# Statistics of x1 in the scan of a Mamba layer: VectorE's bn_stats per row chunk against two accumulating passes on ScalarE

## What is computed

```python
x = x + _L0_conv_ref(_gn(x), ...)     # Mamba: in_proj, conv, selective scan, gate, out_proj
x = x + _L1_conv_ref(_gn(x), m)       # memory of 1024 rows: assign, segment sums, soft read-out

def _gn(v, G=32, eps=1e-5):
    g = v.reshape(B_, G, C_ // G, H_, W_)
    m = jnp.mean(g, axis=(2, 3, 4), keepdims=True)
    s = jnp.var(g, axis=(2, 3, 4), keepdims=True)
    return ((g - m) / jnp.sqrt(s + eps)).reshape(v.shape)
...
def step(h, inp):                     # the selective scan, d = 1024 channels, 16 states
    u_t, d_t, b_t, c_t = inp
    dA = jnp.exp(d_t[..., None] * A)
    dBu = (d_t * u_t)[..., None] * b_t[:, None, :]
    h = dA * h + dBu
    y = jnp.einsum('bdn,bn->bd', h, c_t)
```

## Time and profile before

| | |
|---|---|
| median of 3 runs | 4616.05 us (4615.56 to 4617.21) |
| the profiled execution | 4618.12 us, its span 4616.3 us |
| `scan`: first scan to last gate | 952.64 to 3487.01 us of the span |
| granted clock of TensorE | 0.99 over the span |
| statistics in `scan` (L887) | 64 instructions, 667 ns median |

### The profile page before, as it was taken

The page is one execution under the profiler, slowest core; times in us unless marked ns, Lnnn a source line. Parts: engine busy times, 40 slices in busy tenths (PEclk is TensorE's granted clock), DMA queues, the critical chain, the costliest instruction groups (busy, mean ns, idle before and its releaser), DMA issues. The chain is left out here.

```text
span 4616.3 us, 110600 instructions
## 1 busy us (share of the span) xinstructions
PE 4401.1 (95%) x47036; PEld 2940.8 (64%) x47036; DVE 3880.4 (84%) x4033; ACT 2863.4 (62%) x6005; POOL 2932.5 (64%) x1321
## 2 busy tenths in 40 slices
PE   5999999968999999999999999999997999999999
PEld 4777777745555555555555555555554778777887
DVE  5877677689999999999999999999995777777332
ACT  2666676667777777777777777777763444443111
POOL 1223333269999999999999999999993222222000
PEclk9999999989999999999999999999998999999999
DMA  3555455442233323333332333233321212212543
GB/s 149 207 204 190 165 188 197 170 149 88 84 102 100 100 84 94 100 93 94 102 101 80 96 103 101 83 101 98 97 76 64 83 56 82 83 55 119 199 184 146
DMA packets 195258, 538.60 MB, mean 117 GB/s; under 512 B 15600, under 2 KB 15616, under 8 KB 185680
## 3 DMA queue, kind: packets, MB, share of 16 engines
q1 hardware_dynamic: 189888, 482.41, 31.6%
q0 software_dynamic: 4880, 49.12, 2.7%
HBM read 329.09 MB, written 202.38 MB: 115 GB/s over the span
## 5 line engine op out<-in xcount | busy, mean ns | idle before, releaser
L996 POOL TENSOR_TENSOR sc_hc<-sc_hc,sc_c_rep 128x1024 f32<-128x1024 f32 x1024 | 2390.3, 2383 | 127.0 <-ACT sc_state L1009 102.3
L1191 DVE TENSOR_TENSOR_SCAN sc_hc<-l_m,sc_state,sc_ring 128x512 f32<-128x512 f32 x2048 | 2419.0, 1254 | 11.5 <-PE sc_ring L1118 5.8
L1041 ACT ACTIVATE l_m<-l1s_v,l_neg_a 128x512 f32<-128x512 f32 x2048 | 1351.5, 707 | 6.9 <-DMA l1s_v<-spill 6.8
L1118 PEld LDWEIGHTS sc_ring<-sc_diag,l1s_iota 64*64 64x64 f32 x32768 | 898.5, 133 | 458.4 <-issue 453.2
L1118 PE MATMUL sc_ring<-sc_diag,l1s_iota 64*64 64x128 f32 x32768 | 1042.8, 274 | 45.1 <-DVE sc_hc L1191 41.1
L1128 PE MATMUL sc_y_ps<-sc_hc,sc_fold 128*64 128x512 f32 x4096 | 936.1, 599 | 0.9 <-POOL sc_hc L996 0.9
L1009 ACT ACTIVATE sc_state<-sc_hc 128x2 f32<-128x2 f32 x1024 | 207.1, 202 | 626.0 <-DVE sc_hc L1191 625.8
L1128 PEld LDWEIGHTS sc_y_ps<-sc_hc,sc_fold 128*64 128x64 f32 x4096 | 271.5, 136 | 484.9 <-issue 461.9
L1460 POOL TENSOR_TENSOR l_count<-l_count,as_oh 128x1024 f32<-128x1024 f32 x64 | 184.0, 2875 | 523.4 <-DVE as_oh L1656 523.4
L879 PE MATMUL sc_o_ps<-l_et,l_sums 128*128 128x512 f32 x960 | 464.0, 606 | 4.4 <-ACT sc_b_col L1019 4.4
L70 PE MATMUL fr_mm<-fr_xn_hi,l0f_w_in_hi 128*128 128x512 f32 x1024 | 407.9, 398 | 15.3 <-DVE fr_xn_lo L676 8.6
(11 more groups left out here) (185 smaller groups left out, 5731.1 us busy)
## 6 DMA issues: line engine op xcount, KB each, us to landing
sc_duz<-spill SPq DMA_DIRECT2D x128, 768.0 KB, 6.1
l1s_v<-spill SPq DMA_DIRECT2D x256, 256.0 KB, 4.0
spill<-fr_z SPq DMA_DIRECT2D x64, 512.0 KB, 3.5
spill<-fr_u SPq DMA_DIRECT2D x32, 1024.0 KB, 5.9
spill<-fr_delta SPq DMA_DIRECT2D x32, 1024.0 KB, 5.2
spill<-fr_du SPq DMA_DIRECT2D x32, 1024.0 KB, 6.3
sc_c_rep<-bc SPq DMA_DIRECT2D x128, 256.0 KB, 4.4
soft<-l_et SPq DMA_DIRECT2D x16, 2048.0 KB, 6.2
```

What stands on the lines that cost most here:

```text
L996: nc.gpsimd.tensor_tensor(hc[:, p], hc[:, p], c_rep[:, 2 * q:2 * q + 2, :], ALU.mult).then_inc(s_hp, 1)
L1041: nc.scalar.activation(da[:, p % 4, r, :], delta[:, i % 2, p % 2, :], ACT.Exp, scale=keep.neg_a[:, c:c + 1]).then_inc(s_da, 1)
L1118: done = nc.tensor.matmul(to[:, :, k::4], dut[rows, i % 2, k, HALF * h:HALF * h + HALF], diag[rows, u, 4 * q + c:4 * q + 4:2, k, :], start ...
L1191: nc.vector.tensor_tensor_scan(hc[:, p, r, :], da[:, p % 4, r, :], ring[:, SLOT[at], r::2], state[:, i, 2 * p + r:2 * p + r + 1], ALU.mult ...
```

## The change

In the blocks of `scan` VectorE takes no statistics any more. ScalarE takes them in two steps at the same places of the loops (odd blocks, same tiles m): after the decays of p = 2 the sum over the tile's 512 tokens by an Identity pass with the accumulator (`chunk_mean`), followed by two copies of one column (the mean, and the shift for the next step), and after the decays of p = 5 the sum of squares about that mean by a Square pass with the accumulator (`chunk_variance`), which also raises `s_res`. Both passes write their unused full output to `o_sb`. The five last statistics stay on VectorE, each a `bn_stats` followed by a `bn_aggr` of its own. `keep.mv` holds a mean and a variance for every chunk, and `group_params` puts the second norm's from these by twelve small VectorE instructions that add halves, in place of the eight `bn_aggr`. The first group norm is unchanged.

```diff
-        def statistics(dve, b, j, m):
-            g = b * NJ + j
-            dve.wait_ge(s_sum, KC * g + m + 1)
-            nc.vector.bn_stats(keep.stats[:, b * KC + m, j, :], x_res[:, m % 2, :]).then_inc(s_res, 1)
+        def chunk_mean(act, b, j, m):
+            n = KC * (b * NJ + j) + m
+            act.wait_ge(s_sum, n + 1)
+            nc.scalar.activation(o_sb[:, m % 2, :], x_res[:, m % 2, :], ACT.Identity, accum_out=total[:, 0:1]).then_inc(s_total, 1)
+            act.wait_ge(s_total, n + 1)
+            nc.scalar.activation(keep.mv[:, b * KC + m, j, 0:1], total[:, 0:1], ACT.Copy, scale=1.0 / T).then_inc(s_mean, 1)
+            nc.scalar.activation(total[:, 1:2], total[:, 0:1], ACT.Copy, scale=-ROOT / T).then_inc(s_mean, 1)
+
+        def chunk_variance(act, b, j, m):
+            n = KC * (b * NJ + j) + m
+            act.wait_ge(s_mean, 2 * n + 2)
+            nc.scalar.activation(o_sb[:, m % 2, :], x_res[:, m % 2, :], ACT.Square, bias=total[:, 1:2], scale=ROOT,
+                                 accum_out=keep.mv[:, b * KC + m, j, 1:2]).then_inc(s_res, 1)
+
+        def last_statistics(dve, b, j, m):
+            n = KC * (b * NJ + j) + m
+            dve.wait_ge(s_sum, n + 1)
+            nc.vector.bn_stats(keep.stats[:, m, j, :], x_res[:, m % 2, :]).then_inc(s_taken, 1)
+            dve.wait_ge(s_taken, n - KC * (NG - 1) + 2)
+            nc.vector.bn_aggr(keep.mv[:, b * KC + m, j, :], keep.stats[:, m, j, :]).then_inc(s_res, 1)
...
                             decays(g, i, p)
+                            for at, part in ((2, chunk_mean), (5, chunk_variance)):
+                                if p == at and i in (3, 5, 7) and past:
+                                    part(act, *past[0], i // 2 - 1)
+                                if p == at and i == 1 and len(past) > 1:
+                                    part(act, *past[1], KC - 1)
...
                             recur(g, i, p, 1)
-                            if p == 3 and i in (3, 5, 7) and past:
-                                statistics(dve, *past[0], i // 2 - 1)
-                            if p == 3 and i == 1 and len(past) > 1:
-                                statistics(dve, *past[1], KC - 1)
...
+                def add_halves(t, count, before):
+                    while count > 1:
+                        count //= 2
+                        dve.wait_ge(halved, before)
+                        nc.vector.tensor_tensor(t[:, :, 0:count], t[:, :, 0:count], t[:, :, count:2 * count], ALU.add).then_inc(halved, 1)
+                        before += 1
+                    dve.wait_ge(halved, before)
+
+                nc.vector.tensor_copy(part[:], of_chunks).then_inc(halved, 1)
+                add_halves(part, NJ, 1)
+                nc.vector.scalar_tensor_tensor(away[:], of_chunks[:, :, :, 0], float(NJ), part[:, :, 0:1, 0].broadcast_to([P, n, NJ]),
+                                               ALU.mult, ALU.subtract).then_inc(halved, 1)
+                dve.wait_ge(halved, 5)
+                nc.vector.tensor_tensor(away[:], away[:], away[:], ALU.mult).then_inc(halved, 1)
+                add_halves(away, NJ, 6)
+                nc.vector.scalar_tensor_tensor(mv[:, :, 1], away[:, :, 0], 1.0 / NJ ** 2, part[:, :, 0, 1], ALU.mult,
+                                               ALU.add).then_inc(halved, 1)
```

More of the change, by code:

```diff
@@ L72, in split_matmul, with group_params @@
     return nc.tensor.matmul(out, lhs[0], rhs[1], start=False, stop=stop)
-def group_params(nc, tag, keep, stats, scale, shift, early=()):
+def group_params(nc, tag, keep, stats, scale, shift, early=(), of_chunks=None):
     n = stats.shape[1]
@@ L88, in group_params @@
         step = w.sem("step")
+        halved = w.sem("halved")
+        part = w.sb("part", [P, n, NJ, 2])
+        away = w.sb("away", [P, n, NJ])
         mean_ps = w.sem("mean_ps")
@@ L100, in _ @@
         def _(dve):
-            for i in range(n):
-                nc.vector.bn_aggr(mv[:, i, :], stats[:, i, :, :]).then_inc(step, 1)
-            dve.wait_ge(step, n)
+            if of_chunks is None:
+                for i in range(n):
+                    nc.vector.bn_aggr(mv[:, i, :], stats[:, i, :, :]).then_inc(step, 1)
+                dve.wait_ge(step, n)
+            else:
+                def add_halves(t, count, before):
[14 more added lines that the diff above has]
+                                               ALU.add).then_inc(halved, 1)
+                dve.wait_ge(halved, 10)
+                nc.vector.tensor_scalar(mv[:, :, 1], mv[:, :, 1], 1.0 / NJ, None, ALU.mult).then_inc(step, n - 1)
+                nc.vector.tensor_scalar(mv[:, :, 0], part[:, :, 0, 0], 1.0 / NJ, None, ALU.mult).then_inc(step, 1)
+                dve.wait_ge(step, n)
             nc.vector.tensor_copy(mean[:], mv[:, :, 0]).then_inc(step, 1)
@@ L797, in scan @@
     DIAGS = (1, 1, 1, 2, 2, 1, 1, 0)
+    ROOT = T ** -0.5
     with ExitStack() as ctx:
@@ L808, in scan @@
         o_ps = w.ps("o_ps", [P, T])
+        total = keep.total
         s_w = w.sem("w_out_loaded")
@@ L835, in scan @@
         s_res = w.sem("x1_done")
+        s_total = w.sem("x1_totalled")
+        s_mean = w.sem("x1_mean_done")
+        s_taken = w.sem("last_x1_taken")
         st_x1 = [w.sem(f"x1_stored{i}") for i in range(2)]
@@ L1322, in low @@
                                             ALU.subtract).then_inc(s_lo, 1)
-                statistics(dve, NB - 1, NJ - 2, KC - 1)
+                last_statistics(dve, NB - 1, NJ - 2, KC - 1)
                 dve.wait_ge(s_root, 1)
@@ L1332, in _ @@
                 for m in range(3):
-                    statistics(dve, NB - 1, NJ - 1, m)
+                    last_statistics(dve, NB - 1, NJ - 1, m)
                 for n in range(4):
                     low(n)
-                statistics(dve, NB - 1, NJ - 1, 3)
+                last_statistics(dve, NB - 1, NJ - 1, 3)
                 for n in range(4, 8):
@@ L1855, in program @@
         keep.stats = w.sb("stats", [P, NB * KC, NJ, 6])
+        keep.mv = w.sb("mv", [P, NB * KC, NJ, 2])
+        keep.total = w.sb("total", [P, 2])
         keep.scale = w.sb("scale", [P, NB * KC])
@@ L1895, in program @@
                     scan(nc, keep, d)
-                    group_params(nc, "g2", keep, keep.stats[:], keep.scale[:], keep.shift[:])
+                    group_params(nc, "g2", keep, keep.stats[:], keep.scale[:], keep.shift[:], of_chunks=keep.mv[:])
                     assign(nc, keep, d)
```

## The result

The changed kernel takes 4583.58 us (median of 4 executions, 4578.80 to 4587.27), the kernel before 4616.63 us beside it (4 executions, 4615.56 to 4617.39). The ratio is 0.9928, 95% interval 0.9916 to 0.994: 33 us or 0.72% faster. The profiled execution is the slowest of the four, 4587.27 us, with a span of 4585.5 us. Two executions further down, 6811 us in experiment 7 (the profiled one, mean granted clock 0.61) and 6181 us in experiment 9 (0.68), are in no median and no comparison.

The account below looks back on a forecast made before the run. VectorE was taken to set the pace of `scan`. −34.5 + 0.25 + 0.6 = −33.65 us against the profiled 4618.12 us gave 4584.5, and with the median 2.07 us lower 4582.4 us; range 4579 to 4603 us.

Parts of the forecast that it names:

- VectorE sets the pace, 59 × 0.585 us: In `scan`, 59 bn_stats leave VectorE, the slowest engine, at 0.585 us each: 34.5 us off the path.
- ScalarE is covered: In `scan`, ScalarE's new passes, 1.8 us at 59 places or 106 us, hide in its 538.7 us of waiting for VectorE.
- the 72 us of loss: By the skill's rule alone, moving the statistics to ScalarE would be 106 − 34.5 = 72 us slower.
- GpSimd's waits for `keep_state` vanish: In `scan` from 1200 to 3400 us, GpSimd's 33.0 us of waits for `keep_state` fall under some 10 us.
- the first rival: GpSimd becomes the bound in `scan`, half its `keep_state` waits kept: 21 us lost, about 4603 us; chance 12%.
- The next engine: Over two blocks of `scan`, VectorE at 38.69 us stays slowest, 0.15 us over GpSimd and 0.47 us over TensorE.
- The end: After `scan`, the last statistics' bn_aggr cost +0.25 us and the second norm's parameters in `group_params` +0.6 us.
- Slower, the scans slow down: VectorE's scans slow beside ScalarE's passes over 128x512 tiles: 34 us slower, about 4651 us; chance 5%.
- ScalarE late to VectorE: In block 1, `chunk_mean` delays the decays by 1.05 us, 14 us at most: about 4597 us; chance 4%.
- No change: GpSimd's waits all stay, or a loop through several engines sets the pace: 4616 us; chance 5%.

Follow-up runs that it names:

- experiment 7: The changed kernel with the second scan of p = 3 in every block replaced by a plain multiplication, leaving out that recurrence: 4559.04 us, ratio 0.9874.
- experiment 9: The kernel of experiment 7 run again for a new profile, against the same kernel before: 4558.79 us, ratio 0.9874.
- experiment 1: The changed kernel with the 59 bn_stats put back on VectorE beside ScalarE's passes: 4619.6 us, ratio 1.0005 to the kernel before.
- experiment 2: The changed kernel without any statistics in the scan's blocks, the norm given fixed numbers for them: 4584.17 us, ratio 0.993 to the kernel before.
- experiment 3: The kernel before the change with every bn_stats in the scan's blocks taken twice: 4651.69 us, ratio 1.0075.
- experiment 5: The changed kernel with two more Identity passes on ScalarE, 1.5 us, ahead of `chunk_mean` at each of 59 places: 4584.64 us, ratio 0.993.
- experiment 10: The kernel of experiment 9 with GpSimd's multiplication of p = 3 over only one of the pair's two halves: 4555.32 us, ratio 0.9866.
- experiment 4: The changed kernel once more, unedited: 4584.97 us, ratio 0.993 to the kernel before.
- experiment 6: The changed kernel with five more Identity passes on ScalarE, 3.75 us, ahead of `chunk_mean` at each of 59 places: 4608.83 us, ratio 0.9984.
- experiment 8: The changed kernel with four more 512-column matmuls, result unused, ahead of TensorE's 2.70 us idle time at the first passage: 4585.23 us, ratio 0.9933.

## Why the prediction was right

The forecast was 4582.4 us and the median is 4583.6. The mechanism is as forecast; that the two numbers are only 1.2 us apart is in part luck, as executions of the changed kernel spread over 8 us. By its steps:

- **VectorE sets the pace, 59 × 0.585 us.** Shown: two blocks went from 39.27 to 38.68 us (38.69 forecast), and experiments 1 to 3 put bn_stats at 0.59 us a place, whether it is taken away or doubled.
- **ScalarE is covered.** Shown: taking the passes out gives nothing that can be measured (2), and adding 1.5 us a place costs nothing that can be measured (5). The estimates were 1.05 and 0.75 us, and the parts take 0.94 and 0.70. ScalarE's wait for VectorE fell by 119 us, where I gave about 100; 34 us of it are gone without any pass as well (505.0 us in experiment 2), because VectorE is quicker. The Trainium skill ("ScalarE: Activation LUTs", Rules for kernel authors) puts additions and multiplications on VectorE as the faster engine for them. The rows agree on the price, 1.64 us for 0.58, though the page gives its ratio for bf16 and all data is float32 here. That price falls on an engine with time to spare; the 72 us of loss would need a ScalarE without any.
- **GpSimd's waits for `keep_state` vanish.** 33.0 us became 2.6; "under some 10 us" holds, and they follow VectorE's time (3). They were a consequence of its pace and not a limit, which is what separated the forecast from the first rival at 4603 us. GpSimd's wait for `c_rep` stayed whole, 22.0 us for 20.7, and cost nothing in the chunks.
- **The next engine.** This comparison was too coarse. What bounds the kernel was told by two blocks inside a chunk, with GpSimd 0.15 us and TensorE 0.47 us behind VectorE. Only the first rival counted a whole chunk, and only for GpSimd (154.2 against VectorE's 155.5 us). By the whole chunk VectorE also has its waits at the passage: 20.22 + 19.37 + 6 × 19.34 = 155.6 us now. Experiments 9 and 10 show that TensorE's 154.03 us is the next bound in effect, 1.6 us a chunk or about 24 us in all. Nothing of the forecast hung on it, because both were under VectorE.
- **The end.** The parameters cost +0.66 us for +0.6, the last statistics +0.44 for +0.25. Left out of the sum was the last gate's longer wait, 0.5 to 0.8 us, which is GpSimd's lag behind VectorE at the end of `scan` (experiments 4, 9 and 10). The range had up to 3 us of GpSimd's waits, but spread over the chunks. Together that is 0.8 to 1.1 us more than in the sum, of the 1.2 us between forecast and median; executions of the same kernel spread over more than that.
- **The rivals.** "Slower, the scans slow down" is excluded by experiment 1 (1257 ns against 1254, the time unchanged). "ScalarE late to VectorE" begins only at more than 1.5 us further a place (5, 6). "No change" would have shown idle time of VectorE in its blocks, and there is none.

## What to carry to other kernels

Work that moves from the engine that sets the pace to one with room is worth its distance between starts on the first engine, even if it takes three times as long on the second; check the room at the place itself, not in the sum of waits. Waits of a follower that has caught up with the leader go away when the leader gets faster, so they are no argument that the follower is the next limit; its busy time over a whole period is. Compare engines over a whole period of the loop, passages included: over two blocks this kernel seemed to have 0.15 us left, over a chunk of eight it had 1.4 to 1.6. And look at the end of a stage by itself: a follower's lag that costs nothing inside is paid once at the last step.

## What the runs showed of the hardware

**TensorE's clock after the same idle time.** At the first passage TensorE stood idle for 2.69 or 2.70 us in the profiles of before, of after and of experiments 1 to 6. The 64 matmuls behind it took 1.98 us in experiments 1 to 3 (experiment 1's row stands below), 2.57 in experiment 4, 2.84 in the kernel before, 3.54 and 3.57 in experiments 5 and 6, and 3.69 after the change, where the granted clock was 0.50 as shown above:

```profile
1104.69 1.98 PE L1176 MATMUL sc_ring<-sc_diag,l1s_iota 64*64 64x128 f32 x64 [2.70 <-DVE sc_hc L1249]
```

What decides it is open. With matmuls in place of the idle time (8) they took 1.98 us, in one profile, which experiments 1 to 3 did without them; so that profile doesn't show the cause either.

At the last gate, the eight matmuls behind TensorE's wait for GpSimd took 1.94 us after 0.85 to 1.68 us of idle time (before, after, experiments 1, 2, 4, 8 and 10). After 2.21 us (5) they took 2.97 us, and after 2.67 us 2.90 us in experiment 9 and 3.56 in 6, with a mean granted clock of 0.63, 0.65 and 0.54 over them.

**Accumulating passes.** Over 512 columns Identity and Square with the accumulator cost 0.70 to 0.76 us from start to start, the 0.19 us read of the accumulator included, and neither needs a table load beside Exp.
